# A convolution, attention and mixture-of-experts block on one core: a new table of blocks, and the expert rows added on VectorE

## The chip, the cores and the metric

The kernel runs on one core of one Trainium2 chip, as one launch. The metric is the device time of that launch in microseconds. A core has TensorE (PE in the rows, with PEld for its weight loads), VectorE (DVE), ScalarE (ACT), GpSimd (POOL) and SyncE (SP), which here only issues DMAs.

## What is computed

Eight images of 128 channels and 32 by 32 points go through three layers. Cut to what matters:

```python
# layer 1, per image (S = 1024 points, 128 channels)
x   = group_norm(hidden, pre_g, pre_b) + pos_emb
s   = sigmoid(conv1x1(silu(conv3x3(silu(conv1x1(x))))))      # "spatial weights"
sh  = group_norm(x, norm_g, norm_b)
a   = softmax(q k^T / 4) v          # 8 heads of 16, from sh
m   = two more attentions of width 64; their queries come from x * s
out = group_norm(silu([a, m] @ ff_w1.T + b) @ ff_w2.T @ out_w.T) + hidden
# layer 2, per image, on tokens
t   = t + attention(layer_norm(t))                           # 8 heads of 16
# layer 3, per image
g   = softmax(layer_norm(t) @ gate_w + gate_b); top 2 of 8 experts
t   = t + sum over the 2 experts e of g[e] * (gelu(n @ w1[e] + b1[e]) @ w2[e] + b2[e])
```

The last line is the one whose sum changes its engine: each token gets two rows, each from another expert, times its two gates.

## The kernel before

**Loop.** There is a prologue, a loop of eight turns, and an epilogue. One turn works on several images at once, in four stages: the attention of layer 1 (the conv attention, 32 steps, family `a`), the two wide attentions (16 steps), the experts of the image before (23 tiles), and the token attention of layer 2 (32 steps, family `b`), beside which layer 1 of the next image is prepared (`front`). All engines meet in a barrier at a turn's end. Every engine has its own program (`tensor_program`, `vector_program` and so on), written out by hand, and all read the same tables, so these tables are the schedule.

**Steps.** A step of an attention is, on TensorE, two pairs of score matmuls (`scores`, L869), the weighting of the values (`weigh_values`, L883: eight rows in the trace, four matmuls of 32 columns side by side), and on ScalarE two exponentials of 128x1024 (`exps`, L1137). A row of L883 therefore marks a step. Every eight steps ScalarE copies the finished output out of PSUM (`take_output`, L1129).

**Blocks.** The softmax needs the maximum of each row of scores beforehand. It is made from blocks: TensorE forms a 128x512 piece of scores again in bf16 (`max_block`, L697), into two PSUM banks in turn, and VectorE reduces it (`reduce_block`, L1324). `CONV_BLOCKS` and `TOKEN_BLOCKS` say how many blocks go into each step. Of the 160 blocks that family `a` needs (128 for the heads, 32 for the wide attentions), the first `A_FRONT` are made in the token attention of the turn before and in the prologue, the others in the conv attention. 32 blocks make a unit. When a unit is full, VectorE closes it (L1311), TensorE turns its maxima (a small product `turn_*`, L752), VectorE splits them into three bf16 parts (`split_max`, L1351 to L1355), and SP sends them to DRAM and back into `qs` (`spread_max`, L466 and L469). The scores of steps 8, 16 and 24 wait for one unit each.

**Small products.** `CONV_WINDOW` and `TOKEN_WINDOW` say after which step TensorE does which small product. VectorE takes the last one named for a step a step later. `CONV_EXTRA` and `TOKEN_EXTRA` name VectorE's own work: `stats_e` and `norm_e` (layer norm), `routes`, `slots` (where each token goes), `gates`, and for the next image `start_pre`, `start_x1`, `start_xh`. While it does that, VectorE puts blocks between dependent instructions (`link`, `reduce_next`), up to the step that `look_ahead` allows.

**GpSimd.** In a turn it computes the reciprocal roots (`rstd`, L587), scatters the tokens to the experts (16 indirect DMAs, L620), gathers the experts' rows back (16, L596), then `pre_rstd`, then weighs both sets of rows (L605, two instructions of 128x1024) and adds them to `toke` (L612, two more). After it come `norm_rstd`, the third parts of keys and queries (L638), the twelve instructions that shift the inputs of the 3x3 convolution (`conv_in`, L652 and L654), and `gated`. TensorE's `res0` and `res1` turn the sums of `toke` for the output.

## Time and profile before

| | us |
|---|---|
| median of 3 runs | 3413.22 |
| lowest and highest | 3410.99, 3422.33 |
| profiled execution | 3414.36 |
| its span, first to last instruction | 3412.6 |
| busy in the span: PE, DVE, ACT, POOL | 2881.8 (84%), 2252.0 (66%), 1727.7 (51%), 646.4 (19%) |
| VectorE, blocks of 128x512 (L1324) | 1712 of 684 ns, 1133.0 |
| ScalarE, exponentials of 128x1024 (L1137) | 1024 counted, 996.1 |
| ScalarE, copy of an output (L1129), one | 0.60 |
| TensorE, blocks (L697) and scores (L869) | 687.0 and 646.6 |

A turn takes 392.5 to 395.0 us from its first TensorE instruction to the next turn's. The prologue ends near 110 us and the epilogue begins near 3262 us. The chain of waits that ended last reaches back only to 3264 us, since the barrier before it cuts it, so it tells of the epilogue alone. Inside a turn one has to read stage by stage, which engine waits and for what.

How to read a row of the timeline: start in us, duration in us, engine, line, operation, tiles out<-in, shape, count; in brackets how long the engine was idle before it and what released it. A matmul's duration shows the clock: a value weighting (L883, x8) takes 1.06 us at full clock and about 1.94 at half.

### The profile page before, as it was taken

Reading aid. Unit: us, or ns where it says so; the run is one execution under the profiler, and the core shown is the slowest. Engines: PE = TensorE matmul, PEld = TensorE weight load, DVE = VectorE, ACT = ScalarE, POOL = GpSimd, SP = SyncE. Lnnn points to the kernel's source line nnn. Section 1 sums busy time; section 2 is a strip of 40 time slices with the busy share of each in tenths; the row PEclk is TensorE's granted clock in tenths of the full one; section 3 lists DMA queues with packets and bytes.
Section 4 is the critical chain, followed back from the end, with each engine's and each line's share of the span. In section 5 each row is a group of like instructions: output and inputs, shape, how many; then the busy total and the mean of one; then the engine's idle time right before and its main releaser. Section 6 shows DMA issues by size and latency. Waiting matters only on the chain. (4 is left out here: it accounts for less than half of the span.)

```text
span 3412.6 us, 43675 instructions
## 1 busy us (share of the span) xinstructions
PE 2881.8 (84%) x15494; PEld 1205.3 (35%) x15494; DVE 2252.0 (66%) x4233; ACT 1727.7 (51%) x2591; POOL 646.4 (19%) x558
## 2 busy tenths in 40 slices
PE   4889898989889798898979888897979988898945
PEld 1225332262224432263323622253322622235324
DVE  4665877567774777558775677647775677747740
ACT  1355464555545465554645555553645555454623
POOL 3010322004110320103220140103220041102222
PEclk9799898998999999998999989998999979998967
DMA  4014430163103630153201711044301631026324
GB/s 102 1 37 131 98 64 14 38 185 68 27 14 102 151 63 4 48 161 69 50 14 53 193 45 27 22 140 105 63 13 39 182 72 26 14 87 166 63 71 139
DMA packets 171571, 252.50 MB, mean 74 GB/s; under 512 B 26323, under 2 KB 80287, under 8 KB 171215
## 3 DMA queue, kind: packets, MB, share of 16 engines
q1 hardware_dynamic: 162127, 230.65, 26.9%
q0 software_dynamic: 9216, 18.89, 2.2%
q8 instruction: 133, 2.18, 0.3%
q14 instruction: 95, 0.78, 0.1%
HBM read 192.59 MB, written 56.86 MB: 73 GB/s over the span
## 5 line engine op out<-in xcount | busy, mean ns | idle before, releaser
L1324 DVE TENSOR_REDUCE blockmax<-ps 128x1 f32<-128x512 f32 x1712 | 1133.0, 684 | 438.7 <-PE ps L697 425.6
L1137 ACT ACTIVATE prob<-ps 128x1024 f32<-128x1024 f32 x1024 | 996.1, 1021 | 682.6 <-PE ps L869 666.7
L697 PE MATMUL ps<-ks,qs 96*128 96x512 bf16 x1712 | 687.0, 414 | 212.4 <-DVE blockmax L1324 132.4
L869 PE MATMUL ps<-qs,ks 99*128 99x512 bf16 x2048 | 646.6, 405 | 52.6 <-DMA qs<-maxrow_dram 48.3
L697 PEld LDWEIGHTS ps<-ks,qs 96*128 96x128 bf16 x1712 | 168.2, 102 | 889.2 <-DVE blockmax L1324 688.9
L1181 ACT ACTIVATE prob<-ps,b1t 128x128 f32<-128x128 f32 x828 | 236.7, 369 | 202.8 <-PE ps L970 200.8
L869 PEld LDWEIGHTS ps<-qs,ks 99*128 99x128 bf16 x2048 | 198.5, 103 | 309.8 <-issue 74.5
L587 POOL TENSOR_TENSOR rs<-vn,vec 128x1 f32<-128x1 f32 (+1 forms) x43 | 43.0, 1000 | 1374.3 <-DVE vn L1269 998.8
L883 PE MATMUL ps<-prob,va_b 128*32 128x512 f32 x2048 | 296.5, 653 | 0.0
L883 PE MATMUL ps<-prob,va_a 128*32 128x512 f32 x2048 | 287.3, 634 | 0.0
L1335 DVE TENSOR_REDUCE blockmax<-ps 128x2 f32<-128x1024 f32 x192 | 225.3, 1220 | 40.0 <-PE ps L735 39.0
L596 POOL DMA_INDIRECT routed<-y_dram,slot_u x144 | 136.8, 950 | 512.5 <-DMA y_dram<-prob 471.4
L620 POOL DMA_INDIRECT x_dram<-ta,slot_u x144 | 150.3, 1044 | 362.4 <-DVE slot_u L1557 321.2
L1160 ACT ACTIVATE prob<-ps 128x1024 f32<-128x1024 f32 x128 | 130.2, 1024 | 158.9 <-PE ps L927 93.7
L1321 DVE TENSOR_REDUCE blockmax<-ps 128x2 f32<-128x1024 f32 x128 | 156.9, 1226 | 65.2 <-PE ps L709 59.5
L923 PE MATMUL ps<-routed,km 64*128 64x512 f32 x512 | 144.5, 641 | 4.4 <-ACT prob L1137 4.4
L1643 DVE TENSOR_TENSOR keysum<-keysum,prob 128x1024 f32<-128x1024 f32 x80 | 98.0, 1225 | 74.0 <-ACT prob L1160 73.5
L954 PE MATMUL ps<-prob,vm 128*64 128x512 f32 x512 | 137.3, 614 | 2.7 <-ACT prob L1160 2.7
L1032 ACT ACTIVATE ta<-ps,half_b 128x512 f32<-128x512 f32 (+2 forms) x62 | 42.4, 684 | 127.1 <-PE ps L779 62.1
L1602 DVE RECIPROCAL tb<-ps 128x512 f32<-128x512 f32 x16 | 53.7, 3358 | 64.6 <-PE ps L950 64.6
L709 PE MATMUL ps<-shared 64*128 64x512 bf16 x256 | 49.9, 386 | 45.0 <-DVE blockmax L1321 34.2
L735 PE MATMUL ps<-k_even,parts 32*128 32x512 bf16 x384 | 57.3, 395 | 33.5 <-DVE rowrem L1352 15.6
(227 smaller groups left out, 3363.8 us busy)
## 6 DMA issues: line engine op xcount, KB each, us to landing
shared<-in_w SPq DMA_DIRECT2D x108, 256.0 KB, 3.1
prob<-in_w SPq DMA_DIRECT2D x108, 256.0 KB, 3.3
parts_dram<-parts SPq DMA_DIRECT2D x34, 768.0 KB, 5.2
ks<-parts_dram SPq DMA_DIRECT2D x204, 128.0 KB, 4.6
qs<-parts_dram SPq DMA_DIRECT2D x204, 128.0 KB, 6.8
routed<-in_w SPq DMA_DIRECT2D x90, 256.0 KB, 3.4
xe<-in_w SPq DMA_DIRECT2D x54, 256.0 KB, 3.2
oatt<-in_w SPq DMA_DIRECT2D x54, 256.0 KB, 3.1
```

The costliest lines, as they stand in the source:

```text
L596: pool.indirect_dma_start(out=routed[:, k, t, :], out_offset=None, in_=y_dram, in_offset=bass.IndirectOffsetOnAxis(ap=slot_u[:, k, t:t + 1 ...
L620: pool.indirect_dma_start(out=x_dram, out_offset=bass.IndirectOffsetOnAxis(ap=slot_u[:, k, t:t + 1], axis=0), in_=lnt[:, t, :], in_offset= ...
L697: pe.matmul(ps[:, MX + n % 2, :], qs[0:ROWS, slot, h, tile * P:(tile + 1) * P], ks[0:ROWS, slot, h, cols(k)], start=True, stop=True).then_ ...
L869: mm = pe.matmul(ps[:, SC + h, :], ks[:, slot_of(a, g), h, t * P:(t + 1) * P], qs[:, slot_of(a, g), h, cols(q)], start=True, stop=True)
L883: mm = pe.matmul(ps[32 * j:32 * j + 32, OB, :], va[a][:, t, c:c + 2 * HD], prob[:, n % 3, j, :], start=(t == 0), stop=(t == NT - 1))
L923: pe.matmul(ps[:, SC + 2 * (n % 2) + m, :], km[rows, t * P:(t + 1) * P], qm[rows, cols(q)], start=True, stop=False)
L954: mm = pe.matmul(ps[MD * m:MD * (m + 1), (OB, MX + 1)[q], :], vm[:, t, MD * m:MD * (m + 1)], tile[:, m, :], start=(t == 0), stop=(t == NT ...
L1137: act.activation(prob[:, n % 3, 2 * pr:2 * pr + 2, :], ps[:, SC + 2 * pr:SC + 2 * pr + 2, :], ACT.Exp, scale=HD ** -0.5).then_inc(exp_done ...
L1181: act.activation(hid[i % 2][:, c * P:(c + 1) * P], ps[:, SC + i % 2, c * P:(c + 1) * P], ACT.Gelu, bias=b1t[:, i, c:c + 1]).then_inc(gelu_ ...
L1321: dve.tensor_reduce(cells[:, :, t], ps[:, MX:MX + 2, :], AX.X, ALU.max).then_inc(blocks_used[f], 2)
L1324: dve.tensor_reduce(blockmax[:, unit_of(j), cell_of(j), k:k + 1], ps[:, MX + n % 2, :], AX.X, ALU.max).then_inc(blocks_used[f], 1)
L1335: dve.tensor_reduce(cells[:, h:h + 2, t], early_banks(d), AX.X, ALU.max).then_inc(blocks_used["b"], 2)
```

## The change

- `A_FRONT` is 64 instead of 48: 16 blocks (the second half of unit 1 of family `a`) move from the conv attention to the token attention of the turn before, and to the prologue. The tables of blocks are new: 96 in the conv attention (few beside the layer norm and the routing), 144 in the token attention.
- The windows are moved with them. In the conv attention `turn_a1_1` goes from step 5 to step 0, `turn_a1_2` from 13 to 12, ahead of `slots`, which goes from 12 to 13; `gates` from 14 to 17; the `tro`, `trn`, `logits` products go one step later. In the token attention `start_pre` and `pre` go one step earlier, `turn_b_3` from 20 to 19, `res0` and `res1` to 20 and 21, `c20` to `c31` one step later, `turn_a0_0` from 28 to 26.
- GpSimd only gathers; `pre_rstd` stands after the twelfth gather instead of after the sixteenth. VectorE weighs and adds in one instruction per 128x128 tile (`combine_rows`), four at each of the steps 14 to 17.
- The last `take_output` of the token attention goes behind the barrier, to the head of the next turn.
- SP sends the second group of keys and queries ahead of the output's store.

```diff
-A_FRONT = 48
+A_FRONT = 64
-CONV_EXTRA = {4: ["stats_e"], 5: ["norm_e"], 10: ["routes"], 14: ["gates"]}
+CONV_EXTRA = {5: ["stats_e"], 6: ["norm_e"], 11: ["routes"], 17: ["gates"]}
-TOKEN_EXTRA = {1: ["start_pre"], 3: ["start_x1"], 7: ["start_xh"]}
+TOKEN_EXTRA = {0: ["start_pre"], 3: ["start_x1"], 7: ["start_xh"], 14: ["comb0"], 15: ["comb1"], 16: ["comb2"], 17: ["comb3"]}
-CONV_BLOCKS = (3, 3, 3, 3, 4) + (4,) * 8 + (5, 5, 4, 5, 4, 5, 4) + (4,) * 8 + (0,) * 4
-TOKEN_BLOCKS = (4,) * 4 + (3, 3, 4, 4, 4, 4, 5, 5) + (4,) * 20
+CONV_BLOCKS = (4, 3, 3, 3, 3, 0, 1, 5, 5, 4, 0, 1) + (6, 4, 3, 2, 3, 4, 5, 5) + (4,) * 8 + (0,) * 4
+TOKEN_BLOCKS = (5, 4, 4, 3) + (4,) * 8 + (5, 5, 5, 5, 4, 4, 4) + (5, 5, 5, 5, 6, 6) + (5, 5, 5, 6, 6, 5) + (0,)
...
+                        if token and (k, t) == (1, NT // 2):
+                            rstd("pre_rstd", 1)
                         pool.indirect_dma_start(
...
-                if token:
-                    rstd("pre_rstd", 1)
-                pool.wait_ge(rows_gathered, 16 * ROUTES)
-                pool.wait_ge(done["gate_k"], 1)
-                for k in range(2):
-                    pool.tensor_tensor(routed[:, k, :, :], routed[:, k, :, :],
-                                       gate_k[:, k, :].unsqueeze(2).to_broadcast([P, NT, P]), ALU.mult
-                                       ).then_inc(done["weighted"], 1)
...
-                    pool.tensor_tensor(toke[:, :, :], toke[:, :, :], routed[:, k, :, :], ALU.add
-                                       ).then_inc(done["combined"], 1)
...
-                    pe.wait_ge(done["combined"], 2)
+                    pe.wait_ge(done["combined"], 2 * h + 2)
...
+                elif t == 0 and a == 0:
+                    pe.wait_ge(last_taken, 1)
...
             if experts:
+                act.activation(oatt[:, 3, :], ps[:, OB, :], ACT.Copy).then_inc(last_taken, 1)
...
-                if token:
-                    take_output(1, 3)
...
+            def combine_rows(q):
+                dve.wait_ge(rows_gathered, 16 * ROUTES)
+                for k in range(2):
+                    for t in range(NT // 4 * q, NT // 4 * (q + 1)):
+                        ins = dve.scalar_tensor_tensor(out=toke[:, t, :], in0=routed[:, k, t, :], scalar=gate_k[:, k, t:t + 1],
+                                                       in1=toke[:, t, :], op0=ALU.mult, op1=ALU.add)
...
+                    reduce_next()
+                    if k == 0:
+                        sync()
```

The first place is VectorE in the conv attention, around `split_max` of unit 2 (`maxrow`, `rowrem`). The names `cmp_e`, `tile_*`, `keysum<-b1w` and `b1t` belong to `slots`; `blockmax` is one block; `run_*` belongs to `routes`. Before:

```order
L1563 TENSOR_SCALAR tile_g<-tile_f 128x23
L1324 TENSOR_REDUCE blockmax<-ps 128x1
L1564 CAST tile_e<-tile_g 128x23
L1565 TENSOR_TENSOR cmp_e<-iow,tile_g 128x184
L1324 TENSOR_REDUCE blockmax<-ps 128x1
L1569 TENSOR_TENSOR keysum<-b1w,cmp_e 128x736
L1324 TENSOR_REDUCE blockmax<-ps 128x1
L1571 TENSOR_REDUCE b1t<-keysum 128x92
L1351 CAST maxrow<-ps 16x128
L1352 TENSOR_TENSOR rowrem<-ps,maxrow 16x128
L1354 CAST maxrow<-rowrem 16x128
L1355 TENSOR_TENSOR maxrow<-rowrem,maxrow 16x128
```

After, at the same unit (line numbers are those of the changed kernel):

```order
L1522 TENSOR_TENSOR run_a<-run_b 128x64
L1319 TENSOR_REDUCE blockmax<-ps 128x1
L1346 CAST maxrow<-ps 16x128
L1319 TENSOR_REDUCE blockmax<-ps 128x1
L1347 TENSOR_TENSOR rowrem<-ps,maxrow 16x128
L1319 TENSOR_REDUCE blockmax<-ps 128x1
L1349 CAST maxrow<-rowrem 16x128
L1350 TENSOR_TENSOR maxrow<-rowrem,maxrow 16x128
L1319 TENSOR_REDUCE blockmax<-ps 128x1
L1544 TENSOR_TENSOR cmp_e<-ps,step_e 128x64
```

The split stood behind the whole of `slots`; now it stands ahead of its first instruction.

The second place is GpSimd in the loop, from the scatter to the norm of the next image (`rs<-vn,vec` is a reciprocal root, 128x1 for the group norms). Before:

```order
L620 DMA x_dram<-ta,slot_u 2944x128 x16
L587 TENSOR_TENSOR rs<-vn,vec 128x1
L587 TENSOR_TENSOR rs<-vn,vec 128x8
L596 DMA routed<-y_dram,slot_u 128x128 x16
L587 TENSOR_TENSOR rs<-vn,vec 128x1
L605 TENSOR_TENSOR routed<-routed,gate_k 128x1024 x2
L612 TENSOR_TENSOR toke<-toke,routed 128x1024 x2
L587 TENSOR_TENSOR rs<-vn,vec 128x1
```

After:

```order
L610 DMA x_dram<-ta,slot_u 2944x128 x16
L589 TENSOR_TENSOR rs<-vn,vec 128x1
L589 TENSOR_TENSOR rs<-vn,vec 128x8
L600 DMA routed<-y_dram,slot_u 128x128 x12
L589 TENSOR_TENSOR rs<-vn,vec 128x1
L600 DMA routed<-y_dram,slot_u 128x128 x4
L589 TENSOR_TENSOR rs<-vn,vec 128x1
```

The root for `pre` has moved ahead of four gathers, and the four instructions of 128x1024 are gone.

The third place is VectorE in the token attention from the split of unit 2 of family `b` on. Before, 24 blocks follow it:

```order
L1351 CAST maxrow<-ps 16x128
L1324 TENSOR_REDUCE blockmax<-ps 128x1
L1352 TENSOR_TENSOR rowrem<-ps,maxrow 16x128
L1324 TENSOR_REDUCE blockmax<-ps 128x1
L1354 CAST maxrow<-rowrem 16x128
L1324 TENSOR_REDUCE blockmax<-ps 128x1
L1355 TENSOR_TENSOR maxrow<-rowrem,maxrow 16x128
L1324 TENSOR_REDUCE blockmax<-ps 128x1 x24
```

After, the first two of the four portions that follow it:

```order
L1350 TENSOR_TENSOR maxrow<-rowrem,maxrow 16x128
L1319 TENSOR_REDUCE blockmax<-ps 128x1 x2
L1584 SCALAR_TENSOR_TENSOR toke<-routed,gate_k,toke 128x128 x2
L1319 TENSOR_REDUCE blockmax<-ps 128x1
L1584 SCALAR_TENSOR_TENSOR toke<-routed,gate_k,toke 128x128 x2
L1319 TENSOR_REDUCE blockmax<-ps 128x1 x4
L1584 SCALAR_TENSOR_TENSOR toke<-routed,gate_k,toke 128x128 x2
L1319 TENSOR_REDUCE blockmax<-ps 128x1
L1584 SCALAR_TENSOR_TENSOR toke<-routed,gate_k,toke 128x128 x2
```

Sixteen instructions with two inputs in SBUF have come between the blocks of steps 14 to 17, in pairs with one block between the pairs of a portion.

## Rows read from the trace of the kernel before

**Rows 1.** Windows: us, busy (x) of PE, PEld, DVE, ACT, POOL; PEclk, DMA, GB/s
```profile
2087.00:2221.00 134.00, 110.41 (x603) 35.45 (x603) 95.34 (x219) 70.86 (x81) 18.39 (x17) 0.96 0.07 21
...
2342.00:2480.00 138.00, 121.27 (x589) 37.49 (x590) 101.49 (x180) 79.56 (x93) 49.06 (x41) 0.92 0.33 58
```

**Rows 2.** Timeline of TensorE, conv attention: start us, us, engine, line, operation
```profile
2145.11 1.07 PE L883 MATMUL ps<-prob,va_a 128*32 128x512 f32 x8
...
2149.13 1.06 PE L883 MATMUL ps<-prob,va_a 128*32 128x512 f32 x8
...
2157.28 1.03 PE L869 MATMUL ps<-qs,ks 99*128 99x512 bf16 x2 [5.18 <-DMA qs<-maxrow_dram]
...
2159.95 1.74 PE L883 MATMUL ps<-prob,va_a 128*32 128x512 f32 x8
```

**Rows 3.** Timeline of VectorE at the same place
```profile
2151.57 0.92 DVE L1571 TENSOR_REDUCE b1t<-keysum 128x92 f32<-128x736 f32 x1
...
2153.26 0.28 DVE L1355 TENSOR_TENSOR maxrow<-rowrem,maxrow 16x128 bf16<-16x128 f32 x1
```

**Rows 4.** Timeline of GpSimd, token attention: the thirteenth gather and what follows the sixteenth
```profile
2355.47 0.94 POOL L596 DMA_INDIRECT routed<-y_dram,slot_u  x1 [0.30 <-issue]
...
2360.18 0.59 POOL L587 TENSOR_TENSOR rs<-vn,vec 128x1 f32<-128x1 f32 x1
2361.75 3.75 POOL L605 TENSOR_TENSOR routed<-routed,gate_k 128x1024 f32<-128x1024 f32 x2 [0.97 <-DMA routed<-y_dram,slot_u]
2365.45 6.09 POOL L612 TENSOR_TENSOR toke<-toke,routed 128x1024 f32<-128x1024 f32 x2
```

**Rows 5.** Timeline of VectorE at the same place
```profile
2360.80 0.16 DVE L1273 TENSOR_TENSOR ca<-rs,vec 128x1 f32<-128x1 f32 x1 [3.57 <-POOL rs L587]
...
2362.15 1.50 DVE L1275 TENSOR_TENSOR cb<-vec,nb 128x1 f32<-128x1 f32 x1
...
2364.18 2.39 DVE L1588 SCALAR_TENSOR_TENSOR x<-xin,ca,posw 128x1024 f32<-128x1024 f32 x1
...
2367.10 2.24 DVE L1590 TENSOR_SCALAR x<-x,cb 128x1024 f32<-128x1024 f32 x1
```

**Rows 6.** Timeline of VectorE in the prologue, GpSimd idle: the same three instructions
```profile
21.34 0.16 DVE L1275 TENSOR_TENSOR cb<-vec,nb 128x1 f32<-128x1 f32 x1
21.53 1.28 DVE L1588 SCALAR_TENSOR_TENSOR x<-xin,ca,posw 128x1024 f32<-128x1024 f32 x1
22.85 0.75 DVE L1590 TENSOR_SCALAR x<-x,cb 128x1024 f32<-128x1024 f32 x1
```

**Rows 7.** Timeline of TensorE, token attention, steps 3 and 4
```profile
2361.62 0.61 PE L697 MATMUL ps<-ks,qs 96*128 96x512 bf16 x1 [3.78 <-DVE blockmax L1324]
2362.16 1.94 PE L883 MATMUL ps<-prob,va_b 128*32 128x512 f32 x8
```

**Rows 8.** Timeline of TensorE, token attention: value weightings of three steps in a row
```profile
2389.68 1.06 PE L883 MATMUL ps<-prob,va_b 128*32 128x512 f32 x8
...
2393.38 1.07 PE L883 MATMUL ps<-prob,va_b 128*32 128x512 f32 x8
...
2397.43 1.06 PE L883 MATMUL ps<-prob,va_b 128*32 128x512 f32 x8
```

**Rows 9.** Timeline of GpSimd, token attention: first of twelve instructions in a row
```profile
2416.15 1.24 POOL L652 TENSOR_TENSOR conv_in<-ta,tb 32x496 f32<-32x496 f32 x1 [8.72 <-ACT tb L1028]
```

**Rows 10.** Costliest groups of the page: busy us, mean ns, idle before, releaser
```profile
L1324 DVE TENSOR_REDUCE blockmax<-ps 128x1 f32<-128x512 f32 x1712 | 1133.0, 684 | 438.7 <-PE ps L697 425.6
```

**Rows 11.** Timeline of VectorE in the prologue: one two-input instruction of 128x128
```profile
13.63 0.29 DVE L437 TENSOR_TENSOR ta<-ta,wt 128x128 f32<-128x128 f32 x1
```

**Rows 12.** Timeline of VectorE in the prologue: eight blocks with no attention beside them
```profile
75.08 4.87 DVE L1324 TENSOR_REDUCE blockmax<-ps 128x1 f32<-128x512 f32 x8 [1.44 <-PE ps L697]
```

**Rows 13.** Timeline of GpSimd in the epilogue, behind the last gather
```profile
3396.63 3.74 POOL L605 TENSOR_TENSOR routed<-routed,gate_k 128x1024 f32<-128x1024 f32 x2 [1.62 <-DMA routed<-y_dram,slot_u]
3400.34 4.81 POOL L612 TENSOR_TENSOR toke<-toke,routed 128x1024 f32<-128x1024 f32 x2
```

More of the change, by code:

```diff
@@ L85 @@
 START_WINDOW = {0: ["pre"], 1: ["norm"]}
-CONV_WINDOW = {0: ["tro0"], 1: ["tro1"], 2: ["tro2"], 3: ["tro3"], 5: ["turn_a1_1"], 6: ["trn0"], 7: ["trn1"],
-               8: ["logits"], 9: ["tra0"], 12: ["slots"], 13: ["turn_a1_2"], 16: ["km0"], 17: ["km1"],
-               18: ["tra1", "qm0"], 19: ["qm1"], 20: ["turn_a1_3"], 21: ["trg0"], 22: ["trg1"], 23: ["b20"], 24: ["b21"],
-               25: ["tra2"], 28: ["turn_a1_4"]}
-CONV_EXTRA = {4: ["stats_e"], 5: ["norm_e"], 10: ["routes"], 14: ["gates"]}
+CONV_WINDOW = {0: ["turn_a1_1"], 1: ["tro0"], 2: ["tro1"], 3: ["tro2"], 4: ["tro3"], 7: ["trn0"], 8: ["trn1"],
+               9: ["logits"], 10: ["tra0"], 12: ["turn_a1_2"], 13: ["slots"], 15: ["km0"], 16: ["km1"], 17: ["qm0"],
+               18: ["qm1"], 19: ["tra1"], 20: ["turn_a1_3"], 21: ["trg0"], 22: ["trg1"], 23: ["b20"], 24: ["b21"],
+               26: ["tra2"], 28: ["turn_a1_4"]}
+CONV_EXTRA = {5: ["stats_e"], 6: ["norm_e"], 11: ["routes"], 17: ["gates"]}
 PARTS_WINDOW = {2: ["tra3"], 4: ["tob0"], 6: ["tob1"], 12: ["tg0"], 14: ["tg1"]}
@@ L94 @@
                  11: ["kB"], 12: ["tg4", "qB"], 13: ["vB"], 17: ["tg5"], 25: ["turn_b_0"]}
-TOKEN_WINDOW = {2: ["pre"], 4: ["turn_b_1"], 6: ["norm"], 8: ["kA0"], 9: ["kA1"], 10: ["qA0"], 11: ["qA1"],
-                12: ["turn_b_2"], 13: ["vA0"], 14: ["vA1"], 15: ["c10"], 16: ["c11"], 17: ["vm0"], 18: ["res0"],
-                19: ["vm1", "res1"], 20: ["turn_b_3"], 21: ["c20"], 22: ["c21"], 24: ["c30"], 26: ["c31"],
-                28: ["turn_a0_0"]}
-TOKEN_EXTRA = {1: ["start_pre"], 3: ["start_x1"], 7: ["start_xh"]}
-CONV_BLOCKS = (3, 3, 3, 3, 4) + (4,) * 8 + (5, 5, 4, 5, 4, 5, 4) + (4,) * 8 + (0,) * 4
-TOKEN_BLOCKS = (4,) * 4 + (3, 3, 4, 4, 4, 4, 5, 5) + (4,) * 20
+TOKEN_WINDOW = {1: ["pre"], 4: ["turn_b_1"], 5: ["norm"], 8: ["kA0"], 9: ["kA1"], 10: ["qA0"], 11: ["qA1"],
+                12: ["turn_b_2"], 13: ["vA0"], 14: ["vA1"], 15: ["c10"], 16: ["c11"], 17: ["vm0"], 18: ["vm1"],
+                19: ["turn_b_3"], 20: ["res0"], 21: ["res1"], 22: ["c20"], 23: ["c21"], 25: ["c30"], 26: ["turn_a0_0"],
+                27: ["c31"]}
+TOKEN_EXTRA = {0: ["start_pre"], 3: ["start_x1"], 7: ["start_xh"], 14: ["comb0"], 15: ["comb1"], 16: ["comb2"], 17: ["comb3"]}
+CONV_BLOCKS = (4, 3, 3, 3, 3, 0, 1, 5, 5, 4, 0, 1) + (6, 4, 3, 2, 3, 4, 5, 5) + (4,) * 8 + (0,) * 4
+TOKEN_BLOCKS = (5, 4, 4, 3) + (4,) * 8 + (5, 5, 5, 5, 4, 4, 4) + (5, 5, 5, 5, 6, 6) + (5, 5, 5, 6, 6, 5) + (0,)
 HALVES = {"ff2": ("ff_act", "ff2_half"), "outp": ("ff2", "outp_half"), "tr_x": ("xr", "trx_half"),
@@ L133, in token_blocks @@
     if not token:
-        return turns_of((0,) * 16 + (4,) * 12 + (0,) * 4, late)[n]
+        return turns_of((0,) * 16 + (5, 5, 5, 5, 6, 6) + (5, 5, 5, 6, 6, 5) + (0,) * 4, late)[n]
     return turns_of(TOKEN_BLOCKS, [("b", j) for j in range(B_EARLY, HEAD_BLOCKS)] + late)[n]
@@ L349, in build @@
             "ln_var_e", "ln_rstd_e", "ln_e", "xe", "gate_diff", "gate_exp", "routes", "tile_e",
-            "b1t", "k_even", "slots", "gates", "gate_t", "gate_k", "weighted", "combined")}
-        warmed = sem("warmed")
+            "b1t", "k_even", "slots", "gates", "gate_t", "gate_k", "combined")}
+        warmed, last_taken = sem("warmed"), sem("last_taken")
         out_done = sem("out_done")
@@ L563, in sync_program @@
                     spread_max("b", 3)
+            if front:
+                if token:
+                    sp.wait_ge(pv_done[1], STEPS)
+                for i in range(2):
+                    spread_group(0, i, 1)
             if experts:
@@ L568, in sync_program @@
             if front:
-                if token:
-                    sp.wait_ge(pv_done[1], STEPS)
-                for i in range(2):
-                    spread_group(0, i, 1)
                 spread_max("a0", 0)
@@ L1208, in scalar_program @@
                         small_product(name)
-                if token:
-                    take_output(1, 3)
         def vector_program(dve, conv, experts, token, front, small):
@@ L1666, in vector_program @@
                         reduce_pair(d)
+            if experts and not token:
+                for q in range(4):
+                    combine_rows(q)
             if front and not token:
```

26 lines of the change are left out of this document (17 added, 9 removed).

## The prediction

> **What bounds the kernel now.** The chain of waits that ended last covers only the epilogue, so I read the windows of one turn first, then each engine's waits in them. In the sixth turn the conv attention takes 134 us and the token attention 138 of the turn's 392.5; between them lie 121 us that the change leaves alone [rows 1]. In both attentions TensorE has most of the busy time (110 and 121 us) and VectorE the next most (95 and 101); ScalarE needs 71 and 80. No engine is full. TensorE is held by VectorE, because a block needs one of two PSUM banks, and at a few places by something longer. I looked for these, since the change moves exactly such things.
>
> The longest idle time of TensorE in the conv attention is the wait of step 16 for the row maxima of unit 2: 5.18 us until their DMA has landed [rows 2]. It stands in each of the eight turns, with 5.15 to 5.26 us. The split of these maxima ends at 2153.54, because VectorE first works through all of `slots` up to `b1t` [rows 3]; from there to the scores it is 3.7 us. The step takes 10.8 us from one value weighting to the next, where the step ahead of it took 4.0 [rows 2]. More than the wait itself is lost, because the matmuls behind it run at half the clock: 1.03 us for a pair of scores, and 1.74 for the weighting against 1.07.
>
> In the token attention the longest is at step 3. VectorE waits 3.57 us for `pre_rstd` [rows 5], which GpSimd issues only behind its sixteenth gather [rows 4], and TensorE then waits 3.78 us for a free bank [rows 7]. Behind that comes a second loss. While GpSimd weighs and adds (2361.75 to 2371.5), three instructions of VectorE take 1.50, 2.39 and 2.24 us [rows 5]; the same three took 0.16, 1.28 and 0.75 in the prologue, where GpSimd was idle [rows 6]. That is 3.94 us more, in a stretch in which TensorE again waits for VectorE.
>
> **The change, part by part, for one turn.**
>
> Step 16 of the conv attention. `turn_a1_2` comes a step earlier and its split ahead of `slots`. Unit 2 is then complete after step 11, its split falls to step 13, and the 3.7 us of the round trip end long before step 16, since a step has two exponentials of 0.97 us and so lasts at least 1.9. The gain is 10.8 - 4.0 = 6.8 us. What is late next is the work of `slots`, one step later than before. GpSimd's scatter waits for it, and that is needed only in the experts, a stage later, so nothing is lost there.
>
> Blocks out of the conv attention: 16 fewer in the steps 0 to 19. Where TensorE is the limit, a block costs what the token attention shows: three steps in a row, alike but for four or five blocks, take 3.70 and 4.05 us [rows 8], so 0.35 us. Where VectorE is the limit it costs 0.68 [rows 10]. So 5.6 to 10.9 us. VectorE is nearly full in steps 4 to 14 (layer norm, routing, slots), where ten of the sixteen are taken, but once it is relieved TensorE limits, and in steps 5 and 6, now almost without blocks, TensorE will run ahead and wait for the layer norm. I take 0.4 each: 6.4 us. The conv attention gains 13.2 us.
>
> `pre_rstd` and the shared time. `start_pre` and `pre` come a step earlier and the root stands behind twelve gathers. The thirteenth was issued at 2355.47 [rows 4], so the root can run then, and VectorE, which gets there at 2357.2, has it. The 3.57 us go. With the weighing gone, so do the 3.94. Of the half clock behind these waits (1.94 against 1.07 us for the weighting [rows 7, 8], three times, and the scores between) I take 2 us. Together 9.5; the number of blocks up to step 11 is unchanged. The lower bound is 5, if VectorE, which still has `x1` and its statistics to make here, only becomes late somewhere else; the upper is 12, with all of the half clock.
>
> Blocks into the token attention: 16 more, net, in steps 12 to 31, with five or six where there were four. TensorE is the limit there, so the fifth costs 0.35. A sixth waits for a bank, so I give it VectorE's 0.68. The steps 12 to 15 and 19 to 30 get a fifth block, four of them a sixth, and the last step loses its four, so (16 - 4) x 0.35 + 4 x 0.68 = 6.9. Bounds: 4, and 10.9 at VectorE's price throughout.
>
> Weighing and adding on VectorE: 16 instructions. An instruction with two inputs of 128x128 takes 0.29 us [rows 11], an eighth of the one of 128x1024 is 0.16 [rows 6]; the first is nearer, so 4.6 us, at steps where VectorE had about 1 us free each. But the last two portions fall on the twelve `conv_in` instructions, which keep GpSimd busy for 15.5 us without a gap from 2416.15 on, 1.24 each [rows 9]. The small L1275 waited out the whole of the first L605 (1.50 us instead of 0.16) [rows 4 to 6]. If each of the four pairs in these portions waits once for such an instruction, that is 5 us of VectorE. Of 9.6 us I put 3 on the path. Bounds: 0, if the free time of VectorE takes it all, and 10, if each of the eight waits. `res0` and `res1` come two steps later, and wait for nothing.
>
> The output's copy. ScalarE's 0.60 us no longer stand between the last weighting and the barrier; with its hand-over I take 0.8 us gained. SP's new order moves a store whose landing is awaited only at the barrier, 30 us later: nothing.
>
> One turn: -6.8 - 6.4 - 9.5 + 6.9 + 3.0 - 0.8 = -13.6. Eight turns: -109.
>
> Outside the loop. The prologue makes the 16 blocks too, with no attention to hide them, at 0.61 us each [rows 12], before the last two products of the 3x3 branch: +9.8. The epilogue loses GpSimd's 8.5 us between the gather and `res0` [rows 13]; VectorE's sixteen take 4.6, but `res0` needs only the first half: -5.5.
>
> Sum against the profiled execution: 3414.4 - 109 + 9.8 - 5.5 = 3309.7, which ran 1.1 us above the median. I round to 3310.
>
> **A rule against the change.** The rows show VectorE's two-input and its 1024-wide instructions waiting for GpSimd's [rows 4 to 6]. The Trainium skill says why, in "SBUF — State Buffer", section "SBUF: two separate sides": the two engines share a pair of ports as an exclusive lock, which a VectorE instruction with two SBUF inputs needs as well, and whoever comes second waits for the whole instruction. By this rule the adds of steps 16 and 17 pay for `conv_in` every time. The trace agrees for L1275.
>
> **The rivals.**
>
> Every add beside `conv_in` waits. The engines take turns: 8 x 1.24 = 10 us of VectorE more, all on the path, since its free time is used by the new blocks. Against it: two adds stand directly behind each other, so the second may pass at once. 3310 + 8 x 7 = 3366 (the forecast has 3 of the 10 already).
>
> Conv gains only its wait. TensorE, relieved of blocks, waits instead at `trn0` for the layer norm (some 8 us of VectorE in a row, while two steps without blocks last 2.1 each). Then the 16 blocks bring 1 us instead of 6.4, and the token side its lower bound, 5 instead of 9.5: 3310 + 8 x 9.9 = 3389. Nearly as much, 3310 + 8 x 6.8 = 3364, comes out if the change does not do what it says and step 16 still waits for unit 2. Against that: the order of VectorE puts the split ahead of `slots`.
>
> Both attentions are VectorE's. Then the 16 blocks bring 10.9 in conv, the half clock goes altogether (12 for the start of the token attention), and the late part costs only 4. That gives -6.8 - 10.9 - 12 + 4 + 1 - 0.8 = -25.5 a turn: 3215.
>
> Slower. VectorE becomes the bound of the token attention from step 12 on: 16 blocks at 0.68 (10.9), 16 adds at 0.29 (4.6), and all twelve `conv_in` instructions waited for (15). With the conv side at 7.8 and the start at 5: +30.5 - 12.8 - 0.8 = +16.9 a turn, 3550 at worst. It decides against the change from a cost of 23 us a turn in the late token attention on, where the gains are as forecast, or from 13.1, where they are at their lower ends. For it: six blocks in a step are 4.1 us of VectorE in steps of 3.1 to 4. Against it: VectorE is busy 101 of 138 us there [rows 1], and 11 + 4.6 still fit.
>
> **How the numbers follow.** Forecast 0.66; adds wait 0.10; conv gains only its wait, or still waits, 0.09; VectorE's 0.09; slower 0.06. The range must leave out no more than 2 in 10: the forecast's own bounds (conv 12.4 to 17.7 gained, start 5 to 12, blocks 4 to 10.9, adds 0 to 10) combine to about 7 us a turn either way, 56 us. So 3250 to 3385 holds the forecast, the waiting adds and nearly all of the third case. A measurement of this kernel can tell about 0.3% from no change; faster by more has 0.90, within it 0.04, slower 0.06.
>
> **What would show it.** In the trace of the changed kernel: no L869 that waits 5 us for `qs<-maxrow_dram` (step 16); `ca` (L1268) without 3.6 us of idle time; x1's two instructions at 1.3 and 0.75 us; a conv attention of about 121 us and a token attention of about 137; adds of 0.29 us at steps 14 and 15, and longer ones at 16 and 17. Adds far over 1 us each, a wait at `trn0`, or VectorE without a gap from step 19 to 30 would make it wrong.

## The result and the profile after

The changed kernel takes 3364.98 us (median of 4 runs, 3359.82 to 3369.24), the kernel before 3416.97 (4 runs). The ratio is 0.9848, 95% interval 0.9821 to 0.9874: 1.5% faster, where 3.1% was forecast. The profiled execution took 3359.82 us, its span 3358.0.

The two windows that answer to [rows 1], sixth turn again:

```profile
2059.00:2183.00 124.00, 107.89 (x586) 35.35 (x587) 85.41 (x202) 71.57 (x82) 18.13 (x17) 0.94 0.07 23
2305.00:2445.00 140.00, 123.58 (x605) 38.29 (x604) 114.89 (x212) 79.14 (x92) 39.63 (x37) 0.96 0.31 56
```

The conv attention fell from 134 to 124 us, the token attention rose from 138 to 140. The two long waits that the forecast wanted gone are gone. No scores wait for `maxrow_dram` at step 16 any more, in any of the eight turns. At the start of the token attention VectorE, then GpSimd's root:

```profile
2319.25 0.16 DVE L1268 TENSOR_TENSOR ca<-rs,vec 128x1 f32<-128x1 f32 x1
...
2320.82 0.15 DVE L1270 TENSOR_TENSOR cb<-vec,nb 128x1 f32<-128x1 f32 x1
...
2321.57 1.28 DVE L1601 SCALAR_TENSOR_TENSOR x<-xin,ca,posw 128x1024 f32<-128x1024 f32 x1
...
2323.36 0.82 DVE L1603 TENSOR_SCALAR x<-x,cb 128x1024 f32<-128x1024 f32 x1
```
```profile
2318.65 0.57 POOL L589 TENSOR_TENSOR rs<-vn,vec 128x1 f32<-128x1 f32 x1 [1.12 <-DVE vn L1264]
```

`ca` had 3.57 us of idle time ahead of it in [rows 5] and has none; the three instructions take 0.15, 1.28 and 0.82 us instead of 1.50, 2.39 and 2.24. It is now GpSimd that waits, 1.12 us.

The adds, VectorE first, then the first two GpSimd instructions beside them:

```profile
2371.32 0.61 DVE L1584 SCALAR_TENSOR_TENSOR toke<-routed,gate_k,toke 128x128 f32<-128x128 f32 x2
...
2372.44 2.23 DVE L1584 SCALAR_TENSOR_TENSOR toke<-routed,gate_k,toke 128x128 f32<-128x128 f32 x2
...
2376.39 2.27 DVE L1584 SCALAR_TENSOR_TENSOR toke<-routed,gate_k,toke 128x128 f32<-128x128 f32 x2
...
2379.18 1.94 DVE L1584 SCALAR_TENSOR_TENSOR toke<-routed,gate_k,toke 128x128 f32<-128x128 f32 x2
```
```profile
2371.95 1.25 POOL L642 TENSOR_TENSOR conv_in<-ta,tb 32x496 f32<-32x496 f32 x1 [10.92 <-ACT tb L1024]
2373.28 1.24 POOL L644 TENSOR_TENSOR conv_in<-conv_in,tb 32x496 f32<-32x496 f32 x1
```

A pair alone takes 0.61 us; a pair beside `conv_in` 1.9 to 2.3, that is, 1.3 to 1.7 more, about one GpSimd instruction. In every turn three pairs wait, for 4.7 us together. Taken singly, the adds of the first such pair are

```profile
2372.44 0.92 DVE L1584 SCALAR_TENSOR_TENSOR toke<-routed,gate_k,toke 128x128 f32<-128x128 f32 x1
...
2373.28 1.39 DVE L1584 SCALAR_TENSOR_TENSOR toke<-routed,gate_k,toke 128x128 f32<-128x128 f32 x1
```

where an add alone takes about 0.33 us: each ends 0.15 us behind a GpSimd instruction (those of 2371.95 and 2373.28 end at 2373.20 and 2374.52). So both adds of a pair wait, the second longer than the first, and VectorE and GpSimd take turns. The forecast had one wait of 1.25 us for each of four pairs, 5 us, so its size is right by luck: there are three pairs with two waits each.

So where did the other half of the gain go? The mean of the eight turns, each stage taken from one value weighting to another, gives it. "Start", "adds" and "late" are the token steps 0 to 8, 12 to 18 and 19 to 29 counted from the first weighting; a step's length runs from its weighting to the next one. The wide attentions (42.9 us) and the token steps 9 to 11 (11.2 us) are as before and left out, and the last token step grew from 1.3 to 1.7.

| us | before | after | forecast of the difference |
|---|---|---|---|
| prologue, to the first weighting | 121.9 | 133.7 | +9.8 |
| conv attention | 130.5 | 119.0 | -13.2 |
| experts, to the first token weighting | 84.5 | 86.3 | 0 |
| token attention, start | 43.8 | 34.4 | -9.5 |
| token attention, adds | 28.2 | 33.0 | } +9.9 |
| token attention, late | 42.4 | 49.2 | } |
| last token weighting to next turn | 8.7 | 8.2 | -0.8 |
| epilogue | 151.1 | 144.7 | -5.5 |

The forecast expected 105 us between the two profiled executions and there are 55. By this table the missing 50 lie about equally, with 14 to 17 us over eight turns each, in the conv attention (1.7 a turn too little), in the hand-over from the experts to the token attention (1.8) and behind step 12 of the token attention (2.1, with the last step). The table can't say which part of the change costs what: gains and losses stand in the same rows. That takes kernels with only a part of it.

### The profile page after: what moved, and what is told of

It reads as the page before. It is cut to its first block and busy times, and to the rows that moved or that the text cites. A ratio compares the mean times of both kernels' runs of the same rounds, so it can differ in the third digit from the quotient of the medians.

```text
span 3358.0 us, 43826 instructions
## 1 busy us (share of the span) xinstructions
PE 2872.1 (86%) x15510; PEld 1206.7 (36%) x15510; DVE 2296.0 (68%) x4395; ACT 1728.0 (51%) x2592; POOL 565.1 (17%) x522
## 3 DMA queue, kind: packets, MB, share of 16 engines
q8 instruction: 133, 2.18, 0.3%
## 5 line engine op out<-in xcount | busy, mean ns | idle before, releaser
L863 PE MATMUL ps<-qs,ks 99*128 99x512 bf16 x2048 | 628.0, 398 | 6.8 <-ACT prob L1133 5.8
L879 PE MATMUL ps<-prob,va_b 128*32 128x512 f32 x2048 | 286.3, 632 | 5.3 <-ACT prob L1133 5.3
L1330 DVE TENSOR_REDUCE blockmax<-ps 128x2 f32<-128x1024 f32 x192 | 225.4, 1221 | 45.3 <-PE ps L726 44.3
L589 POOL TENSOR_TENSOR rs<-vn,vec 128x1 f32<-128x1 f32 (+1 forms) x43 | 42.9, 998 | 1253.1 <-DVE vn L1264 884.6
L600 POOL DMA_INDIRECT routed<-y_dram,slot_u x144 | 144.0, 1000 | 516.3 <-DMA y_dram<-prob 476.1
L1028 ACT ACTIVATE ta<-ps,half_b 128x512 f32<-128x512 f32 (+2 forms) x62 | 42.4, 684 | 169.8 <-PE ps L771 82.5
L1584 DVE SCALAR_TENSOR_TENSOR toke<-routed,gate_k,toke 128x128 f32<-128x128 f32 x144 | 80.2, 598 | 24.3 <-DMA routed<-y_dram,slot_u 24.1
```

The lines of the kernel that those rows point to most:

```text
L600: pool.indirect_dma_start(out=routed[:, k, t, :], out_offset=None, in_=y_dram, in_offset=bass.IndirectOffsetOnAxis(ap=slot_u[:, k, t:t + 1 ...
L863: mm = pe.matmul(ps[:, SC + h, :], ks[:, slot_of(a, g), h, t * P:(t + 1) * P], qs[:, slot_of(a, g), h, cols(q)], start=True, stop=True)
L879: mm = pe.matmul(ps[32 * j:32 * j + 32, OB, :], va[a][:, t, c:c + 2 * HD], prob[:, n % 3, j, :], start=(t == 0), stop=(t == NT - 1))
L1330: dve.tensor_reduce(cells[:, h:h + 2, t], early_banks(d), AX.X, ALU.max).then_inc(blocks_used["b"], 2)
```

## The experiments

Eleven kernels ran, each with the kernel before timed beside it. The latter's median was between 3419 and 3425 beside these eleven and 3417 beside the changed kernel, so the ratios given are to it. Differences between two versions in us can be off by some 8 us for this reason; stages are taken from one profiled execution each.

**First, which part does what.** Four kernels: the early split alone; VectorE's adds with the order at the start of the token attention and the output's copy, but the old blocks; both together; and the changed kernel with its adds earlier.

turn_only:

```
 A_FRONT = 48
-... 12: ["slots"], 13: ["turn_a1_2"], ...
+... 12: ["turn_a1_2"], 13: ["slots"], ...
-CONV_BLOCKS = (3, 3, 3, 3, 4) + (4,) * 8 + (5, 5, 4, 5, 4, 5, 4) + (4,) * 8 + (0,) * 4
+CONV_BLOCKS = (4,) * 28 + (0,) * 4
```

> The kernel before with one part of the change: turn_a1_2 at step 12 and slots at 13, and the blocks of conv steps 0 to 19 spread as four per step (80 in sum as before), so that unit 2 is complete after step 11. All else is as before. Theory A (the wait of step 16 is worth the 6.8 us that step was longer than its neighbour): conv attention about 124 us instead of 130.5, 3417 - 8 x 6.8 = 3363. Rival B (TensorE only reaches another wait on VectorE, which is nearly full in steps 4 to 14): the conv attention keeps 2 to 3 us of it, 3390 to 3400.

Measured: ratio 0.9882 (0.9863 to 0.9901), 3380.64 us, between the two. The conv attention took 125.0 us on average (before 130.5), its steps 12 to 18 33.6 instead of 39.7. The place gained 6.1 us, so theory A held there; 0.6 us a turn each were lost in steps 0 to 8 and in the experts, 0.7 behind the token attention, and 1.8 once in the prologue, where the edit changes only one block.

weigh_old_table is the changed kernel with the old `CONV_WINDOW`, `CONV_EXTRA` and `CONV_BLOCKS`, with `turn_b_3`, `res0` and `turn_a0_0` at steps 20, 19 and 28 of the token attention, the old prologue table, and with

```
-A_FRONT = 64
+A_FRONT = 48
-TOKEN_BLOCKS = (5, 4, 4, 3) + (4,) * 8 + (5, 5, 5, 5, 4, 4, 4) + (5, 5, 5, 5, 6, 6) + (5, 5, 5, 6, 6, 5) + (0,)
+TOKEN_BLOCKS = (4,) * 4 + (3, 3, 4, 4, 4, 4, 5, 5) + (4,) * 20
```

> The changed kernel with the old number of blocks in front (48) and the old tables of the conv attention: VectorE weighs and adds at steps 14 to 17, the root stands behind twelve gathers, the output's copy lies behind the barrier. turn_a1_2 is late as before. Theory A (the parts add up as the changed kernel's step rows show: start of the token attention -9.4, hand-over from the experts +1.5, adds +3.3, barrier -0.5 a turn, epilogue -6.5): 3417 - 41 - 6.5 = 3369. Rival B (with four blocks in a step VectorE has room, the adds cost nothing): 3343. Rival C (the adds beside conv_in cost all of their waits, 4 pairs x 1.6 us, with four blocks too): 3390.

Measured: 0.9845 (0.9829 to 0.9862), 3366.12 us; theory A. Token attention 119.0 us (before 127.0): start 33.2, adds 30.8, late 42.5.

weigh_turn_48 is the same kernel with the edit of turn_only on top.

> The changed kernel with 48 blocks in front instead of 64, four per step in both attentions; turn_a1_2 at step 12 ahead of slots as in the changed kernel. It is the changed kernel without the move of 16 blocks. Theory A (the move is a loss: a block gives back 0.32 us in the conv attention, costs 0.51 in the token attention, and 0.74 once in the prologue): 3365 - 8 x 3.1 - 11.8 = 3328. Rival B (as the forecast had it, 6.4 gained and 6.9 lost a turn, 9.8 in the prologue): 3365 - 4 - 9.8 = 3351. Rival C (without the move the step after turn_a1_2 waits for VectorE, so that conv gains no more than 3 us): 3365 or above.

Measured: 0.9693 (0.9676 to 0.9710), 3313.74 us. **Without the move of the sixteen blocks (and the windows that go with it) the change is worth 3.1%, and with it 1.5%.** That this is the 3.1% of the forecast is chance: the forecast was for the kernel with the move. All three theories, A the least, had the price of the move too low. By stages, 48 against 64 blocks in front: conv attention 124.2 to 119.0, so 5.2 us gained; token attention 118.9 to 129.5, so 10.6 lost; experts 0.6 lost; prologue 126.1 to 133.7. The token attention in four stretches (start, steps 9 to 11, adds, late), windows of the version with 48 and of the changed kernel, same columns as above:

```profile
2277.00:2311.00 34.00, 30.49 (x157) 8.69 (x159) 28.57 (x62) 19.39 (x22) 10.76 (x11) 0.97 0.27 45
2311.00:2322.00 11.00, 10.99 (x59) 3.47 (x55) 10.41 (x19) 8.50 (x12) 3.46 (x3) 1.00 0.18 74
2322.00:2352.00 30.00, 25.95 (x151) 10.54 (x149) 27.44 (x49) 19.33 (x26) 15.79 (x13) 1.00 0.41 80
2352.00:2395.00 43.00, 41.15 (x205) 11.55 (x207) 31.85 (x56) 26.84 (x32) 5.08 (x4) 1.00 0.30 51
```
```profile
2312.00:2347.00 35.00, 31.87 (x158) 9.20 (x160) 28.93 (x63) 19.17 (x21) 10.12 (x11) 0.92 0.23 40
2347.00:2358.00 11.00, 10.67 (x54) 3.31 (x48) 10.00 (x18) 8.37 (x12) 3.46 (x3) 1.00 0.20 77
2358.00:2391.00 33.00, 27.36 (x154) 10.81 (x153) 30.41 (x54) 19.45 (x25) 15.79 (x13) 1.00 0.37 71
2391.00:2440.00 49.00, 44.55 (x214) 12.75 (x213) 38.76 (x68) 26.01 (x32) 5.07 (x4) 1.00 0.27 45
```

The late stretch grows by 6 to 7 us at full clock, and VectorE's busy time in it by 6.9.

adds_early:

```
-14: ["comb0"], 15: ["comb1"], 16: ["comb2"], 17: ["comb3"]
+10: ["comb0"], 11: ["comb1"], 12: ["comb2"], 13: ["comb3"]
```

> The changed kernel with the four portions at steps 10 to 13 instead of 14 to 17, ahead of all of conv_in. Blocks, order of everything else and sums are the same. Theory A (four pairs of adds take 1.6 us more each beside conv_in, and about 2.5 of these 6.4 us a turn end up on the path): adds of 0.30 us on average, token steps 12 to 18 30.5 us instead of 33.0, 3365 - 20 = 3345. Rival B (the fifth block holds those steps, not the adds): adds as short, but the steps the same length, 3360 to 3368.

Measured: 0.9836 (0.9813 to 0.9860), 3362.64 us: rival B, no difference. The adds, one of 128x128 each, fell from 598 to 450 ns on average:

```profile
L1584 DVE SCALAR_TENSOR_TENSOR toke<-routed,gate_k,toke 128x128 f32<-128x128 f32 x144 | 59.0, 450 | 24.3 <-DMA routed<-y_dram,slot_u 24.1
```

That is 2.6 us of VectorE a turn (they now meet three other GpSimd instructions, and a pair beside one takes 1.0 to 1.5 us). Steps 12 to 18 took 28.4 us, but steps 9 to 11 took 14.9 instead of 11.2. The token attention gained 0.8 us, the experts 1.3, and the conv attention lost 2.0, at half clock (below). So the waits beside GpSimd's instructions are real, and of 2.6 us less the token attention shows 0.8. How much of them was on the path is not isolated, since the adds also have other blocks around them there.

**Second, why a block is so dear.** In the code of a step of the token attention the blocks stand so: block, score pair, block, score pair, block, weighting, and behind it the fourth and all further ones; then the next step's first. With five or six, three or four stand in a row for two banks. I call a step bare when TensorE does no small product in it. A late bare step of six blocks in the changed kernel, TensorE and then VectorE:

```profile
2433.43 1.06 PE L879 MATMUL ps<-prob,va_b 128*32 128x512 f32 x8
2434.43 0.60 PE L688 MATMUL ps<-ks,qs 96*128 96x512 bf16 x2
2435.60 0.39 PE L688 MATMUL ps<-ks,qs 96*128 96x512 bf16 x1 [0.57 <-DVE blockmax L1319]
2436.20 0.39 PE L688 MATMUL ps<-ks,qs 96*128 96x512 bf16 x1 [0.21 <-DVE blockmax L1319]
...
2437.82 1.06 PE L879 MATMUL ps<-prob,va_b 128*32 128x512 f32 x8
```
```profile
2434.85 3.77 DVE L1319 TENSOR_REDUCE blockmax<-ps 128x1 f32<-128x512 f32 x6 [0.62 <-PE ps L688]
```

and a bare step of four in the version with 48 (2377.51 to 2380.66), VectorE:

```profile
2378.94 2.52 DVE L1318 TENSOR_REDUCE blockmax<-ps 128x1 f32<-128x512 f32 x4 [0.63 <-PE ps L688]
```

Both steps are 0.63 us in which VectorE has an empty pair of banks (during the weighting), plus 0.63 for each block without a gap: 4.39 and 3.15 us. VectorE sets the pace, though it is busy only 80 to 86% of the step. Is that so because of the place of the extra blocks, because of VectorE's pace, or TensorE's? Three kernels tell.

blocks_apart, in `attention_step`:

```
+                more = len(blocks) - 4 if a else 0
+                cuts = [0, 1, 3 if more > 1 else 2]
+                cuts.append(cuts[2] + (2 if more > 0 else 1))
...
-                for f, j in blocks[1:2]:
+                for f, j in blocks[1:cuts[2]]:
...
-                for f, j in blocks[2:3]:
+                for f, j in blocks[cuts[2]:cuts[3]]:
...
-                for f, j in blocks[3:]:
+                for f, j in blocks[cuts[3]:]:
```

> The changed kernel with one difference: in a step of the token attention with five or six blocks TensorE no longer issues the extra ones behind the weighting, where they stand in one row with the first block of the next step (three or four behind each other for two banks), but one between the two score pairs (where there are six) and one ahead of the weighting. Numbers of blocks, their order and VectorE's work are the same. Theory A (an extra block costs what it does, 0.45 to 0.6 us, because it is the third in a row and waits for VectorE to free a bank): token steps 19 to 29 go from 49.2 to about 45 us and 12 to 18 from 33.0 to 32, 5 us a turn, 3365 - 40 = 3325. Rival B (VectorE's pace of 0.6 us per block is the limit wherever they stand): 3358 to 3368, the waits only move.

Measured: 1.0038 (1.0025 to 1.0051), 3436.85 us: slower than the kernel before, and neither theory. The token attention took 135.5 us instead of 129.5, and the conv attention, whose code is the same, 2.9 more. A bare step of six stayed as it was, 4.3 us, so its order was not the reason for its price. Other steps grew, above all the two with the 3x3 branch's products (in the sixth turn from 5.8 and 7.0 to 7.7 us each) and the one with `c31` (3.9 to 6.5). TensorE there:

```profile
2448.64 2.75 PE L771 MATMUL ps<-conv_in,sa2w 96*16 96x512 f32 x6
...
2454.12 0.39 PE L688 MATMUL ps<-ks,qs 96*128 96x512 bf16 x1 [0.80 <-DVE blockmax L1322]
2454.72 0.39 PE L688 MATMUL ps<-ks,qs 96*128 96x512 bf16 x1 [0.20 <-DVE blockmax L1322]
2455.04 1.07 PE L879 MATMUL ps<-prob,va_b 128*32 128x512 f32 x8
```

During 2.75 us of products VectorE runs dry again (2.31 us idle), and then more blocks at VectorE's pace stand ahead of the weighting. That they cost less behind it is my reading and not shown.

short_maxima, in `reduce_block`:

```
+                    wide = HALF // 2 if f == "a0" else HALF
-... ps[:, MX + n % 2, :], AX.X, ALU.max
+... ps[:, MX + n % 2, 0:wide], AX.X, ALU.max
```

> The changed kernel, where the row maxima of the 64 blocks computed ahead for the next conv attention (prologue and late token attention) are taken over the first 256 of their 512 columns only, so that part of that computation is left out. TensorE's work and order are the same; only VectorE's instruction for such a block falls from 0.61 to about 0.38 us. Theory A (VectorE's pace sets the price of a block: a step of six lasts 0.62 us in which VectorE has nothing, and 6 x 0.63; TensorE alone would need 0.22 for a block): token steps 19 to 29 from 49.2 to about 44 us, 8 x 5, and 64 x 0.23 = 15 in the prologue: 3365 - 55 = 3310. Rival B (TensorE sets the price): token attention unchanged, only the prologue's 15: 3350.

Measured: 0.9756 (0.9738 to 0.9773), 3342.55 us. TensorE does the same work, and the late stretch fell from 49.2 to 45.3 us. Bare steps of six in it are 3.9 us instead of 4.4, and VectorE no longer runs without gaps:

```profile
2417.55 0.75 DVE L1320 TENSOR_REDUCE blockmax<-ps 128x1 f32<-128x256 f32 x2 [0.89 <-PE ps L688]
...
2418.46 0.76 DVE L1320 TENSOR_REDUCE blockmax<-ps 128x1 f32<-128x256 f32 x2 [0.16 <-PE ps L688]
```

So VectorE's pace is the price in the changed kernel (theory A's mechanism), but a second limit lies close below it: six blocks cost VectorE 1.4 us less, and the step gained 0.5, as VectorE now waits for TensorE between blocks. The total stayed 1% above A's figure, nearer to rival B's: the token attention gained 4.3 us a turn and the prologue 9.0, but the conv attention gave 2.9 back and the end of the turn 1.3.

token_shape_48 moves three blocks from bare steps to steps with a small product, in the version with 48 and the conv table of shape_48 (below):

```
-... (4,) * 20
+... (4,) * 12 + (3, 5, 3, 5, 5, 3, 4, 4)
```

> The version with 48 blocks in front and the reshaped conv table, with the token steps 24 to 31 at (3, 5, 3, 5, 5, 3, 4, 4) blocks in place of four each: fewer in steps without a small product, more in those with one. Sum and all else are the same. Theory A (in a bare step a block costs VectorE's 0.63 us; beside a small product of 1.02 us on TensorE the fifth costs 0.2 to 0.35): three blocks moved, 0.3 each or about 1 us a turn: 3299 - 8 = 3291. Rival B (the price is the same everywhere): 3299. Either is near to what the measurement can tell, so the steps in the profile decide.

Measured: 0.9627 (0.9609 to 0.9644), 3296.41 us. The steps decide: three bare ones went from 3.4, 3.1 and 3.1 to 2.8, 2.6 and 2.6 us, the two beside `c30` and `c31` from 3.7 to 3.9, the one beside the split from 4.3 to 4.9. A block is worth 0.55 in a bare step and costs 0.2 beside a product of 1.02 us, in one and the same attention. The late stretch is 0.6 us shorter for it; steps 12 to 18, which the edit leaves alone, are 0.6 longer, so that the token attention is 118.9 us in both.

**Third, the other terms.** adds_out:

```
-                    for t in range(NT // 4 * q, NT // 4 * (q + 1)):
-                        ins = dve.scalar_tensor_tensor(out=toke[:, t, :], ...)
...
+                    if k == 1:
+                        dve.memset(toke[:, 2 * q, 0:1], 0.0).then_inc(done["combined"], 1)
```

> The changed kernel without the weighing and adding: the sixteen instructions of a turn are left out (a memset of one column per portion carries the signal), so that the output lacks the experts' rows. It gives the price of the adds on the path. Theory A (what the same steps show with four blocks each, 28.3 us before and 30.6 with the adds): steps 12 to 18 go from 33.0 to 30.7, 8 x 2.3 = 18 us, and some 3 in the epilogue: 3344. Rival B (all the 9.6 us that the adds take beside conv_in are on the path): 3290. Rival C (the blocks fill the time anyway): 3360.

Measured: 0.9734 (0.9717 to 0.9752), 3335.02 us: the adds cost 30 us in all by the times, 39 by the ratios. Steps 12 to 18 took 27.7 us instead of 33.0, the whole token attention 124.7 instead of 129.5, and the conv attention 1.0 more. The adds hold VectorE for 9.4 us a turn (80.2 us in all, 4.6 of them in the epilogue), so about half, 4.8 us, is on the token attention's path. Theory A is the nearest in the total, but in its own steps it had 2.3 us, and they gave 5.3: an add costs more where there are five blocks than where there are four.

start_late puts `start_pre` and `pre` a step back:

```
-TOKEN_WINDOW = {1: ["pre"], ...      -TOKEN_EXTRA = {0: ["start_pre"], ...
+TOKEN_WINDOW = {2: ["pre"], ...      +TOKEN_EXTRA = {1: ["start_pre"], ...
```

> The changed kernel with start_pre at step 1 and pre at step 2 of the token attention, as before the change; root behind twelve gathers as changed. Theory A (the hand-over from the experts grew by 2 us because VectorE's two statistics of 1.28 us come ahead of the first blocks, while TensorE waits for a bank): experts to the first weighting 84.8 us instead of 86.4, 3365 - 12 = 3353. Rival B (the hand-over is long where TensorE still has half its clock there, whatever VectorE does first): no change at that place. Rival C (the root, a step later, holds the last four gathers and x1 back): the start of the token attention grows by 2 us or more, 3380.

Measured: 0.9873 (0.9851 to 0.9896), 3380.39 us: rival C. The start took 36.4 us instead of 34.4. The hand-over was 84.8 us in five turns and 86.2 in three; adds_early, which has the changed kernel's order there, had 85.0 throughout. So VectorE's order there, which is the same in the changed kernel and in adds_early, does not by itself make it long.

shape_48 is weigh_turn_48 with other conv steps:

```
-CONV_BLOCKS = (4,) * 28 + (0,) * 4
+CONV_BLOCKS = (5, 5, 5, 4, 2, 2, 4, 5, 5, 5, 2, 4) + (5, 4, 3, 3, 4, 4, 4, 5) + (4,) * 8 + (0,) * 4
```

> The version with 48 blocks in front (VectorE weighs and adds, turn_a1_2 early), with the conv attention's first 80 blocks moved out of the steps in which VectorE is full: (5, 5, 5, 4, 2, 2, 4, 5, 5, 5, 2, 4) in steps 0 to 11 and (5, 4, 3, 3, 4, 4, 4, 5) in 12 to 19 in place of four per step. Theory A (steps 4, 5, 9 and 15 are VectorE's, so a block fewer there gives 0.6 us and one more elsewhere costs 0.35): conv attention 121 us instead of 124, 3314 - 24 = 3290. Rival B (an extra block costs VectorE's 0.6 in the other steps too, being third in a row): 3308 to 3320.

Measured: 0.9628 (0.9610 to 0.9645), 3299.42 us, between the two theories: conv attention 122.3 instead of 124.2. Steps 12 to 18 gained 3.3 us, steps 0 to 8 lost 2.0.

shape_40 goes on to 40 blocks in front:

```
-A_FRONT = 48
+A_FRONT = 40
-TOKEN_WINDOW = {... 28: ["turn_a0_0"]}
+TOKEN_WINDOW = {... 29: ["turn_a0_0"]}
-CONV_BLOCKS = (5, 5, 5, 4, 2, 2, 4, 5, 5, 5, 2, 4) + ...
+CONV_BLOCKS = (6, 5, 5, 5, 3, 3, 5, 6, 5, 5, 4, 4) + ...
-TOKEN_BLOCKS = ... + (4,) * 20
+TOKEN_BLOCKS = ... + (4,) * 8 + (4, 4, 4, 3, 3, 4, 3, 4, 3, 3) + (3, 2)
```

> The same version with 40 blocks in front instead of 48: eight blocks more in steps 0 to 11 of the conv attention, eight fewer in the late token attention (bare steps down to three, the last to two), turn_a0_0 a step later. Theory A (a block costs 0.63 us in bare token steps and about 0.35 in the conv attention, 0.74 in the prologue): 3299 - 8 x 8 x 0.28 - 6 = 3275. Rival B (VectorE is full in conv steps 4 to 11, so a block costs 0.6 there as well): 3293. Rival C (the unit closes too late for the next conv attention, whose first step then waits for the row maxima): above 3310.

Measured: 0.9674 (0.9656 to 0.9692), 3311.79 us, no gain, and 0.5% lost against shape_48. In the profiled execution, which was the fastest of its four (3293.74 us; the others took 3308 to 3318), the token attention is 3.0 us shorter and the conv attention 3.2 longer, for eight blocks each: 0.38 and 0.40 a block. With these tables, moving blocks stops paying there. **The best versions are shape_48 and token_shape_48, 3.7% below the kernel before;** the two can't be told apart by time.

## Why the prediction was wrong by half

Both waits went as it said. The sum failed on the moved blocks: their price in the token attention was read from the wrong kind of step, and what they do to the hand-over and the start was put at nothing.

- Step 16: forecast -6.8, measured -6.7 (40.1 to 33.4 us in steps 12 to 18, weigh_old_table to weigh_turn_48). The wait and its size are right; that nothing is lost behind it is not, and the sum agrees by luck. The step with the wait gained 7.5 us (10.8 to 3.3), the two behind it lost 3.0, and the other steps gained 2.2, four of which have a block fewer. In the first of the two TensorE waits 2.18 us for VectorE, which is at the end of `slots` and at `gates`; in the second a product takes 1.91 us, 1.02 at full clock. The wait, in weigh_turn_48:

```profile
2090.69 0.39 PE L688 MATMUL ps<-ks,qs 96*128 96x512 bf16 x1 [2.18 <-DVE blockmax L1318]
```

- Start of the token attention: forecast -9.5, measured -9.4, and -10.5 without moved blocks. Right, with the wait and VectorE's three instructions as read; the 2 us for the half clock were not measured apart.
- Adds: forecast +3.0 on the path, measured +2.3 with four blocks in a step (28.2 to 30.6) and 4.8 by leaving them out where there are five. Within its bounds; but adds and fifth blocks share VectorE, so their prices are not two separate terms.
- Blocks out of the conv attention: forecast -6.4, measured -5.2, a figure into which the clock enters (last section). The rival had named a reason: in the changed kernel steps 6 and 11 last 10.7 and 8.0 us, since TensorE runs through the empty steps and waits for VectorE's layer norm and routing. A wait at `trn0` was one of the signs against the forecast, and the second row is one:

```profile
2084.52 0.39 PE L688 MATMUL ps<-ks,qs 96*128 96x512 bf16 x1 [2.29 <-DVE blockmax L1319]
...
2087.85 1.09 PE L731 MATMUL ps<-wt,ta 128*128 128x128 f32 x4 [1.36 <-DVE ta L1293]
```

- **Blocks into the token attention: forecast +6.9, measured +10.6** (weigh_turn_48 to the changed kernel). This is the step that failed, with 30 of the 50 us missing. From step 19 on the forecast had 5.5 and it is 7.1; in steps 12 to 15, where the adds are too, it had 1.4 and it is 2.4 (steps 12 to 18); steps 0 to 8 get two blocks more and steps 10 and 11 two fewer, for which it had nothing, and it is 1.1, as steps 9 to 11 gave nothing back. The price of a fifth block, 0.35 us, was read from [rows 8]. Behind the first two of those weightings stands a product of 1.02 us, in the kernel before for instance

```profile
2390.91 1.02 PE L744 MATMUL ps<-xh,wt 128*128 128x512 f32 x2
```

and there TensorE is the limit: it has no idle time between these weightings. In bare steps VectorE's pace is, with four blocks already (3.15 us with four, 4.39 with six, 0.62 a block). "TensorE is the limit there" was taken from busy times (121 against 101 us in [rows 1]) and from a kind of step that the late ones are not. The bound of 10.9, "VectorE's price throughout", comes near the total, but not for its reason: beside a product a block costs 0.2 to 0.35, and 1.1 of the 10.6 lie in the start.
- Hand-over from the experts: forecast nothing, measured +1.8 (14 us in all). From the first block of step 0 to the first weighting the kernel before needs 7.03 us in six turns and 5.85 in two, 6.7 on average, the version with 48 blocks 7.22 and the changed one 7.86. So 0.6 is the fifth block of step 0 and 0.5 comes with the rest of the change; 0.7 more is lost before that first block. TensorE's clock takes part: the first weighting, 1.06 us at full clock and 1.94 at half, takes 1.53 on average before and 1.90 after. What keeps the clock low there longer is open.
- Barrier -0.8 and epilogue -5.5, measured -0.5 and -6.4: right.
- Prologue +9.8, measured +11.8: 7.6 for the sixteen blocks, 0.48 each, and 4.1 that weigh_old_table has too, with no block more. The cause of these 4.1 is open; turn_only has 1.8 of them, though its edit touches the prologue in one block only.

The rivals at 3364 and 3366 hit the measured time, and neither is what happened. Step 16 no longer waits. Of the waiting adds the mechanism is there, as each of six adds a turn waits and the second of a pair doesn't pass at once, but they wait for 4.7 us where the rival had 10 on the path, and all the adds together cost about 5. From the total alone either would have passed as confirmed.

VectorE's waits beside GpSimd (0.61 and 2.23 us for the same two instructions) agree with the rule of the Trainium skill that was weighed against the change ("SBUF — State Buffer", section "SBUF: two separate sides"). They did not decide against the change: adds_early removed 2.6 us of them a turn, and the time stayed the same.

## What to carry to other kernels

Price a unit of work in the kind of step into which it goes, by taking one such step apart: if an engine's instructions stand there without a gap between two idle pieces of fixed length, it sets the pace, at whatever busy share. With only two banks between two engines, as here, a long instruction of the first (a weighting, a product) leaves the second with nothing to do, and in the steps above this time wasn't made up. And split a change before judging it: this one was a gain of 3.1% and a loss of 1.6% in one. Nor does a total that agrees confirm a sum: two of the terms here, step 16 and the adds' waits, came out right through errors that cancel.
